# A mixture of experts, second stage of one kernel: the gate and up products one expert further ahead, two buffers for the sum, sequences written out

## The reference

```
x = hidden_states.reshape(-1, H)                      # H = 256
scores = sigmoid(x @ gate_w.T)                        # 8 experts
# groups of 2 experts, the 2 best groups, in them the 4 best experts
cw = 2.5 * topk_w / (sum(topk_w) + 1e-20), spread over the 8 experts
g = einsum('nh,ehi->eni', x, Wg); u = einsum('nh,ehi->eni', x, Wu)   # I = 128
y = einsum('eni,eih->enh', silu(g) * u, Wd)
out = einsum('enh,ne->nh', y, cw) + mlp(x, Wg_s, Wu_s, Wd_s)
```

## Time and profile before

| | |
|---|---|
| median of 3 runs | 4768.33 us |
| profiled execution | 4779.36 us, span 4777.4 us |
| TensorE matmul busy | 4059.4 us (85%) |
| VectorE busy | 2999.0 us (63%) |
| ScalarE busy | 2449.4 us (51%) |
| GpSimd busy | 2220.0 us (46%) |
| mean granted clock of TensorE | 0.95 |
| the mixture, from its first gate product to its last sum | 1876.4 to 2656.0 us |

### The profile page before, as it was taken

One profiled execution on the slowest core, in us unless ns is written; L12 is line 12 of the kernel. 1 busy time (PEld: TensorE's weight loads), 2 busy tenths in 40 slices (PEclk: granted clock), 3 DMA queues, 4 the chain that ended last, 5 costly groups with the idle time before them and its releaser, 6 DMA issues. The chain is left out here.

```text
span 4777.4 us, 147918 instructions
## 1 busy us (share of the span) xinstructions
PE 4059.4 (85%) x60532; PEld 3227.1 (68%) x60628; DVE 2999.0 (63%) x7236; ACT 2449.4 (51%) x5553; POOL 2220.0 (46%) x2255
## 2 busy tenths in 40 slices
PE   3888898888888885888888599999999999998668
PEld 2776677677767775777777366666676666666656
DVE  2777777777776775777777555555555555554455
ACT  3545555555555442333333366666666666666335
POOL 4666666666666650000000155555554555555354
PEclk8999999999999997999999799999999999999669
DMA  2222222221222121000000211111111111110233
GB/s 82 56 48 57 67 48 52 66 60 46 53 67 58 44 48 49 27 18 18 27 18 22 78 28 28 28 28 28 28 31 31 46 28 28 28 28 23 101 125 111
DMA packets 173293, 221.53 MB, mean 46 GB/s; under 512 B 32349, under 2 KB 117472, under 8 KB 171232
## 3 DMA queue, kind: packets, MB, share of 16 engines
q1 hardware_dynamic: 166160, 195.49, 15.5%
q0 software_dynamic: 6480, 16.92, 1.0%
HBM read 68.35 MB, written 44.19 MB: 24 GB/s over the span
## 5 line engine op out<-in xcount | busy, mean ns | idle before, releaser
L1591 POOL TENSOR_TENSOR c_prob<-c_prob,c_inv 128x512 f32<-128x512 f32 (+1 forms) x512 | 482.6, 947 | 648.8 <-DVE c_inv L1875 639.1
L1680 ACT ACTIVATE c_prob<-c_s_ps,c_nmax 128x256 f32<-128x256 f32 (+1 forms) x1024 | 459.2, 464 | 156.6 <-DVE c_nmax L1870 155.3
L1870 DVE TENSOR_REDUCE c_nmax<-c_s_ps 128x2 f32<-128x512 f32 (+1 forms) x512 | 316.8, 619 | 265.9 <-PE c_s_ps L2080 263.6
L848 POOL TENSOR_TENSOR a_swap<-a_swap,a_sin 128x512 f32<-128x512 f32 x128 | 204.9, 1600 | 533.0 <-DMA a_swap<-a_raw 533.0
L212 POOL TENSOR_TENSOR b_var<-b_mv,b_eps 128x4 f32<-128x4 f32 x16 | 8.5, 533 | 696.6 <-DVE b_mv L304 696.5
L889 ACT COPY a_raw<-a_w_ps 128x512 f32<-128x512 f32 x256 | 150.3, 587 | 332.1 <-PE a_w_ps L74 331.7
L1691 ACT COPY c_pT<-c_t_ps 128x512 f32<-128x512 f32 (+1 forms) x512 | 280.5, 551 | 50.0 <-PE c_ab_ps L2112 49.9
L2092 PE MATMUL c_t_ps<-c_ident,c_prob 128*128 128x128 f32 x1792 | 284.6, 275 | 21.8 <-ACT c_pT L1691 16.1
L1170 PE MATMUL a_w_ps<-a_mem,a_sT 64*32 64x65 f32 x14848 | 216.1, 226 | 94.7 <-issue 91.2
L2092 PEld LDWEIGHTS c_t_ps<-c_ident,c_prob 128*128 128x128 f32 x1792 | 214.5, 141 | 101.4 <-POOL c_prob L1591 36.2
L2080 PE MATMUL c_s_ps<-c_k,c_q 128*128 128x512 f32 (+1 forms) x512 | 272.6, 532 | 3.5 <-ACT c_prob L1680 3.5
(11 more groups left out here) (407 smaller groups left out, 13508.9 us busy)
## 6 DMA issues: line engine op xcount, KB each, us to landing
a_swap<-a_raw SPq DMA_DIRECT2D x1024, 64.0 KB
c_k<-c_aoT_hi SPq DMA_DIRECT2D x86, 128.0 KB, 2.4
c_k<-c_aoT_lo SPq DMA_DIRECT2D x86, 128.0 KB, 2.4
c_k<-c_stage SPq DMA_DIRECT2D x84, 128.0 KB, 2.3
d_xb<-sorted_rows SPq DMA_DIRECT2D x71, 130.0 KB
a_x_ln<-x SPq DMA_DIRECT2D x128, 64.0 KB, 2.1
a_acc<-x SPq DMA_DIRECT2D x64, 128.0 KB
after_attn<-a_acc SPq DMA_DIRECT2D x64, 128.0 KB, 2.5
```

Source lines behind the costliest of these rows:

```text
L848: nc.gpsimd.tensor_tensor(q_sw, q_sw, table(sin), ALU.mult)
L1591: nc.gpsimd.tensor_tensor(p, p, inv[:, n % 4].unsqueeze(2).to_broadcast([P, 2, KB])[:, :, keys_of(i)], ALU.mult).then_inc(norm_ready, 1)
L1680: last = nc.scalar.activation(prob[:, n % 4, h, keys_of(i)], s_ps[:, n % 2, h, keys_of(i)], ACT.Exp, bias=nmax[:, n % 4, h:h + 1], accum_o ...
L1870: nc.vector.tensor_reduce(nmax[:, n % 4], s_ps[:, n % 2, :, keys_of(i)], AX.X, ALU.max, negate=True).then_inc(max_ready, 1)
```

## The change

The gate and up products run three experts ahead of the down product instead of two. ScalarE's copy and silu and VectorE's low part and multiply are issued one expert earlier, with VectorE's sum in front of them; the first two experts' steps move ahead of the first body. The sum `acc` gets a second buffer, chosen by the sequence's parity, and `stored` becomes two semaphores. `steps` writes out all 16 sequences, so that every wait compares with a constant.

```diff
 def steps(eng, body):
-    body(0, 0)
-    with eng.Fori(0, NSEQ // 2 - 1) as turn:
-        body(turn * 2 + 1, 1)
-        body(turn * 2 + 2, 0)
-    body(NSEQ - 1, 1)
+    for it in range(NSEQ):
+        body(it, it % 2)
...
-    AHEAD = 2
+    AHEAD = 3
...
-        acc = sb("acc", [P, T, D])
+        acc = sb("acc", [P, 2, T, D])
...
-        stored = sem("stored")
+        stored = [sem(f"stored{k}") for k in range(2)]
...
-                sp.dma_start(sequence(dst_v, it), acc[:]).then_inc(stored, 16)
+                sp.dma_start(sequence(dst_v, it), acc[:, par]).then_inc(stored[par], 16)
...
             silu(0, 0, 0)
+            h_hi_copy(0, 0, 0)
+            silu(0, 0, 1)
             def body(it, par):
                 for e in range(E):
-                    h_hi_copy(it, par, e)
-                    if e + 1 < E:
-                        silu(it, par, e + 1)
-                    elif not last_step(it):
-                        silu(it + 1, 1 - par, 0)
+                    for stage, later in ((h_hi_copy, e + 1), (silu, e + 2)):
+                        if later < E:
+                            stage(it, par, later)
+                        elif not last_step(it):
+                            stage(it + 1, 1 - par, later - E)
...
-                    if e == 0 and t == 0 and not first_step(it):
-                        dve.wait_ge(stored, it * 16)
+                    if e == 0 and t == 0 and it >= 2:
+                        dve.wait_ge(stored[par], it // 2 * 16)
...
             times_up(0, 0, 0)
+            h_lo_sub(0, 0, 0)
+            times_up(0, 0, 1)
             def body(it, par):
                 order.step(it)
                 for e in range(E):
-                    h_lo_sub(it, par, e)
                     if e:
                         accumulate(it, par, e - 1)
-                    if e + 1 < E:
-                        times_up(it, par, e + 1)
-                    elif not last_step(it):
-                        times_up(it + 1, 1 - par, 0)
+                    for stage, later in ((h_lo_sub, e + 1), (times_up, e + 2)):
+                        if later < E:
+                            stage(it, par, later)
+                        elif not last_step(it):
+                            stage(it + 1, 1 - par, later - E)
```

More of the change, by code:

```diff
@@ L196, in body @@
                 sp.wait_ge(acc_done, (it + 1) * T * E)
-                sp.dma_start(sequence(dst_v, it), acc[:]).then_inc(stored, 16)
+                sp.dma_start(sequence(dst_v, it), acc[:, par]).then_inc(stored[par], 16)
             steps(sp, body)
-            sp.wait_ge(stored, 16 * NSEQ)
+            for k in range(2):
+                sp.wait_ge(stored[k], 16 * NSEQ // 2)
         @block.gpsimd
@@ L395, in accumulate @@
                         dve.wait_ge(y_ready, (it * E + e) * YB + t // BT + 1)
-                    if e == 0 and t == 0 and not first_step(it):
-                        dve.wait_ge(stored, it * 16)
+                    if e == 0 and t == 0 and it >= 2:
+                        dve.wait_ge(stored[par], it // 2 * 16)
                     if e and t == 0:
                         dve.wait_ge(acc_done, (it * E + e) * T)
-                    into = x_in[:, par, t, :] if e == 0 else acc[:, t, :]
+                    into = x_in[:, par, t, :] if e == 0 else acc[:, par, t, :]
                     if e < E0:
-                        nc.vector.tensor_tensor(acc[:, t, :], y_ps[:, t, :], into, ALU.add).then_inc(acc_done, 1)
+                        nc.vector.tensor_tensor(acc[:, par, t, :], y_ps[:, t, :], into, ALU.add).then_inc(acc_done, 1)
                     else:
-                        nc.vector.scalar_tensor_tensor(acc[:, t, :], y_ps[:, t, :], cw[:, par, t, e - E0:e - E0 + 1], into, ALU.mult, ALU.add).then_inc(acc_done, 1)
+                        nc.vector.scalar_tensor_tensor(acc[:, par, t, :], y_ps[:, t, :], cw[:, par, t, e - E0:e - E0 + 1], into, ALU.mult, ALU.add).then_inc(acc_done, 1)
             stats_of(0, 0)
```

## The result

The changed kernel takes 4717.53 us (median of 4, 4716.31 to 4719.25); the kernel before, 4773.1 us (median of 4 with the run added beside it, 4767.22 to 4794.73). The ratio is 0.9891, 95% interval 0.9865 to 0.9918: faster by 1.1%, about 52 us by the ratio. The forecast was 4736, 32 us less than before, with a range from 4712 to 4757: the sign and that range held, the gain was about 20 us larger, and the narrower range from the bounds of its own terms, 4722 to 4750, was missed.

What follows compares the result with a forecast made beforehand. The mixture was taken as bound by TensorE, with gains only in its waits: 28.7 + 1 + 0 + 4 - 2 + 0 = 31.7, so 32 us off 4768.3 gives 4736; range 4712 to 4757, own range 4722 to 4750.

Steps and rivals of the forecast that it cites:

- Experts 5 and 7: TensorE's waits for VectorE's sums before these down products: each 0.69 us shorter in 15 sequences, as h_lo moves behind the sum.
- expert 1: TensorE's wait for expert 0's sum: 0.57 of 2.85 us shorter, 14 times; the rest stays with the late load.
- the end of the stage: Last two experts' down products, with no gate/up between them: 1 us of gain, between -1 and 3.
- The second buffer: Second sum buffer removes expert 0's sum's wait for the store, already over before the statistics begin: worth 0.
- The case that the buffer matters: Rival: the bubble at expert 1 goes, 32 us, and the clock's 22 with it: about 4682; chance 0.03.
- Groups written out: Seven loop turns removed from the mixture: 4 us gained, between 0 and 7.5, less 2 for bringing in more code.
- The 2 for code: Cost of 23 more instruction packets for TensorE in the written-out mixture: 2 us, bounds 1.6 and 34.
- The clock: TensorE's granted clock after the expert-1 wait: taken as 0, between 22 us gained and 1.7 lost.
- the clock's case: Rival: idle spells of 2.3 us at expert 1 no longer lower the clock, 22 us more: about 4714; chance 0.14.
- VectorE was indeed full: Rival: VectorE, without slack between sums of experts 4 and 6, waits for ScalarE; 11 us left, about 4757; chance 0.15.
- Code loading: Rival: TensorE's and VectorE's queues wait at each new code block, 58 us for 23 packets: 4792, slower; chance 0.06.

Runs made afterwards that it cites:

- The held border: The changed kernel plus one idle vector addition, about 0.6 us, behind the statistics before each expert-1 wait: 4728.86 us, ratio 0.9953 to the kernel before.
- the last run: The changed kernel with SyncE's load issued ahead of the store and VectorE's routing cut into shorter, spread pieces: 4624.35 us, ratio 0.9737 to the kernel before.

## Why the prediction came out as it did

- *Experts 5 and 7, 20.7 us; expert 1, 8.0 us.* Right: the sums are measured at 21.0 and 6.3, with waits of 0.84, 0.85 and 2.26 us where 0.75, 0.75 and 2.3 were forecast. The 21.0 hold 0.9 from the end of the stage, forecast at 1, and some 2 that belong to writing out, as the run that only writes out shows.
- *The second buffer, 0.* Right: 731.7 against 731.4 us. The case that the buffer matters would have taken the whole bubble away; the bubble at expert 1 did come from the order of two transfers on SyncE's list, not from a missing buffer, and moving the load removed it.
- *Groups written out, 4 - 2 = 2 us.* Mis-sized: it measured 12.2 alone and 13.3 on top of the order. Alone, the 4 should have been the whole 7.5 and 2 for the later sums. On top of the order it is another sum, since the order already covers h_lo: 5.0 of idle time, 5.9 of clock and 2.4 of other busy time. The 2 for code should have been 0: the changed kernel brought the 30 packets of the forecast, and no matmul in the mixture waits for issue:

```profile
q8 instruction: 30, 0.49, 0.3%
```

- *The clock, 0.* Mis-sized, and the largest part of the miss: 10.3 of the 13.3 us of busy time. I took each border to bring the clock down whether the wait was 2.85 or 2.3 us. In 6 us windows from the end of each of the 14 border waits, the granted clock is below 0.9 in 10 before, three of them at 0.50 throughout; in 7 after, none of them lower than 0.72. The held border has 11 again, and 8.2 us of busy time with them.
- Sum by measured terms: 34.9 of idle time (forecast 33.7), 0 for code (forecast -2), 10.3 of clock (forecast 0) and 3.0 of other busy time (no term): 48.2, where 32 was forecast. The result lies within the range because the range reaches past the clock's case, not because the sum was right.
- *The rivals.* The clock's case, 4714, was nearer to the result than the forecast, though only three of the ten falls went and 10.3 of the 22 us. VectorE was indeed full between the sums of experts 4 and 6, 9.55 us with hardly a gap (2186.52 to 2196.07, where it was 10.22), but h_lo waited for ScalarE only twice, 1.4 us, so it took nothing back. Code loading didn't decide.

What writing out does to the clock is only in part understood. Alone it saves none; on top of the order it saves 5.9 us. In the loop 10 of the 14 border waits are followed by the lower clock against 7, and five of the ten stand behind a turn, which fits, but no run holds the turns' length by itself. The 2.4 us of busy time on top of the order, and 3.6 alone, that go with the loop and not with the clock stay open.

## What to carry to other kernels

Where a busy engine waits behind an in-order list, ask which piece ahead of the awaited instruction doesn't have to be there, and how long the longest piece is against the time that one step leaves: cutting pieces of 2.7 to 2.8 us to about 1.5 or less was worth 31.5 us once the load came early, nearly as much as the change's whole reordering, 34.6. Price a shorter wait of TensorE twice, once by its length and once by the clock behind it. Read the second from the stretches at the lower clock; the busy time of the same matmuls alone overstates it (13.3 against 10.3 here, 6.6 against none in the last run). When a transfer is late, look at what stands ahead of it on its queue before giving its neighbour a second buffer.

## What the hardware showed that I had not expected

Border waits of the same length end either way. In the changed kernel one of 2.23 us before 2120.22 was followed by the lower clock and one of 2.26 us before 2167.02 was not:

```profile
2120.22:2123.72 3.50, 3.50 (x16) 3.21 (x17) 3.50 (x10) 0.62 (x1) 0.58 (x1) 0.61 0.00 0
2167.02:2170.52 3.50, 3.50 (x21) 3.15 (x22) 3.50 (x10) 0.62 (x1) 0.58 (x1) 1.00 0.00 0
```

Sixteen matmuls against 21 ran in those 3.5 us. Length alone doesn't decide it in the other runs either: in the changed kernel's repeat a wait of 1.93 us was followed by the lower clock, and in the run that only writes out one of 3.06 us was not. A wait of this kind has an expected price, not a fixed one; what decides a single case isn't shown here.
